# Gated group norms ahead of a column scan: the group statistics about the last mean, a shorter reciprocal root, copies in pieces, more filler matmuls

## The reference

```python
def gated(v, cfc_w, bn_w, bn_b):          # layers 0 to 2: x = x + gated(gn(x), ...)
    mean, mx, std = mean(v), max(v), std(v, ddof=1)      # over the 1024 pixels of a channel
    u = stack([mean, mx, std], -1)                       # 4 x 1024 x 3
    med = median(u.reshape(4, -1), axis=-1)              # of 3072 values per image
    z = einsum('bck,ck->bc', (u - med) ** 3, cfc_w)
    g = sigmoid(z / sqrt(1 + 1e-5) * bn_w + bn_b)
    return v * g

def scan(v, conv_w, conv_b, a):           # layer 3: x = x + scan(gn(x), ...)
    # forward, then backward over the 32 columns:
    # cur = prelu(Wc @ prev + conv_b) + column, Wc 1024 x 1024
```

## Time and profile before

| | us |
|---|---|
| median of 3 runs | 903.53 |
| lowest and highest | 901.96, 905.42 |
| profiled execution | 902.32 |
| its span in the profile | 900.6 |
| loading and first statistics | up to 57.9 |
| gated layers with the last group norm | 57.9 to 144.2 |
| column scan | from 144.2 |

### The profile page before, as it was taken

The page is one execution under the profiler, slowest core; times in us unless marked ns, Lnnn a source line. Parts: engine busy times, 40 slices in busy tenths (PEclk is TensorE's granted clock), DMA queues, the critical chain, the costliest instruction groups (busy, mean ns, idle before and its releaser), DMA issues.

```text
span 900.6 us, 13037 instructions
## 1 busy us (share of the span) xinstructions
PE 807.3 (90%) x3699; PEld 632.0 (70%) x3699; DVE 688.5 (76%) x1410; ACT 433.8 (48%) x1380; POOL 36.3 (4%) x68
## 2 busy tenths in 40 slices
PE   0055569999999999999999999999999999999996
PEld 0022226888888888888888888888888888888885
DVE  7987777677666766776667678877887887788887
ACT  6974441444444444444444444444444444444444
POOL 2002430000000000000000000000000000000002
PEclk9996667999999999999999999999999999999998
DMA  8940020000000000000000013333222333332223
GB/s 349 421 166 1 0 94 24 1 0 0 0 0 0 0 0 0 0 0 0 0 0 0 0 47 93 93 93 93 87 72 74 93 93 93 93 93 80 72 80 116
DMA packets 71513, 56.79 MB, mean 63 GB/s; under 512 B 1872, under 2 KB 67408, under 8 KB 69456
## 3 DMA queue, kind: packets, MB, share of 16 engines
q1 hardware_dynamic: 71072, 56.63, 18.9%
q10 hardware_dynamic: 432, 0.07, 0.0%
HBM read 39.91 MB, written 16.78 MB: 63 GB/s over the span
## 4 chain that ended last, share of the span: by engine, by line
PE 85%; DVE 12%; issue 1%; ACT 1%; DMA 1%; ACTq 0%; DVEq 0%
PE ps_prods L544 26%; PE ps_prods L547 25%; PE ps_prods L548 25%; PE ps_turns L556 6%; DVE half_max L624 4%; DVE below_flags L676 3%; DVE bn_parts L619 2%; PE ps_values L511 1%; DMA x_sb<-x_cols 1%; DVE under L682 0%; DVE x_sb L774 0%; PE ps_second L492 0%; DVE t L606 0%; DVE rstd L608 0%; DVE t L607 0%
## 5 line engine op out<-in xcount | busy, mean ns | idle before, releaser
L544 PE MATMUL ps_prods<-w_hi,s_hi 128*128 128x512 f32 x992 | 402.3, 406 | 0.5 <-DVE s_lo L764 0.5
L547 PE MATMUL ps_prods<-w_lo,s_hi 128*128 128x512 f32 x992 | 401.4, 405 | 0.0
L548 PE MATMUL ps_prods<-w_hi,s_lo 128*128 128x512 f32 x992 | 391.1, 394 | 0.0
L456 ACT ACTIVATE act_buf<-ps_prods 128x256 f32<-128x256 f32 x248 | 81.9, 382 | 358.7 <-PE ps_prods L548 355.7
L774 DVE SCALAR_TENSOR_TENSOR x_sb<-act_buf,x_sb 128x256 f32 (+1 forms) x248 | 107.2, 432 | 156.4 <-ACT act_buf L462 145.8
L544 PEld LDWEIGHTS ps_prods<-w_hi,s_hi 128*128 128x128 f32 x992 | 186.9, 188 | 39.3 <-DVE s_lo L764 1.3
L548 PEld LDWEIGHTS ps_prods<-w_hi,s_lo 128*128 128x128 f32 x992 | 187.2, 189 | 38.4
L547 PEld LDWEIGHTS ps_prods<-w_lo,s_hi 128*128 128x128 f32 x992 | 187.6, 189 | 32.8
L462 ACT ACTIVATE act_buf<-ps_turns,bias 128x128 f32<-128x128 f32 x496 | 157.6, 377 | 50.8 <-PE ps_turns L556 50.8
L468 ACT ACTIVATE ps_below<-ps_turns,neg_bias 128x128 f32<-128x128 f32 x496 | 153.0, 362 | 0.0
L781 DVE SCALAR_TENSOR_TENSOR x_sb<-ps_below,neg_slope,x_sb 128x256 f32 (+1 forms) x248 | 119.3, 481 | 4.9
(11 more groups left out here) (120 smaller groups left out, 320.9 us busy)
## 6 DMA issues: line engine op xcount, KB each, us to landing
x_sb<-x_cols SPq DMA_DIRECT2D x16, 1024.0 KB, 21.3
stage<-x_cols SPq DMA_DIRECT2D x31, 512.0 KB, 4.0
out_cols<-x_sb SPq DMA_DIRECT2D x31, 512.0 KB, 4.8
w_raw<-w_t SPq DMA_DIRECT2D x8, 512.0 KB, 21.3
x_sb<-x_cols SPq DMA_DIRECT2D x1, 2048.0 KB, 8.0
x_sb<-x_cols SPq DMA_DIRECT2D x1, 512.0 KB, 3.8
out_cols<-x_sb SPq DMA_DIRECT2D x2, 256.0 KB, 2.3
params<-gates ACTq DMA_DIRECT2D x1, 60.0 KB, 5.5
```

Source lines behind the costliest of these rows:

```text
L456: act.activation(act_buf[:, half], ps_prod[c][:, half], ACT.Copy).then_inc(raw_copied, 1)
L544: pe.matmul(ps_prod[c], s_hi[:, k, :], w_hi[:, k, w_cols], start=(k == 0), stop=False)
L547: pe.matmul(ps_prod[c], s_hi[:, k, :], w_lo[:, k, w_cols], start=False, stop=False)
L548: return pe.matmul(ps_prod[c], s_lo[:, k, :], w_hi[:, k, w_cols], start=False, stop=(k == CT - 1))
```

## The change

- **Group norm.** The second moment is no longer taken about the new group mean but about the last one, so that mean and second moment come out of one product (64 columns instead of 32), and the variance follows by subtracting the square of the mean's shift. Layer 0 keeps its two products (`first_norm`). The later ones (`next_norm`) scale the centred arrays `cent` by 1 + gate x rstd.
- **Second moment.** Its two squares and their sum, `cent[:, 0]`, are formed in the rounds 0 to 2 of the median search, behind the comparison (L682).
- **rsqrt** has eight dependent operations instead of ten, with other constants.
- **Copies.** ACT and DVE copy the means and maxima in pieces of 2, 2 and 4 channel tiles, and PE transposes means and maxima of a piece in turn; the deviations come last.
- **Small steps.** `under_steps` is one instruction, and `halves` is gone: `fold` is scaled once at the start and `middle` itself is the stationary operand of the last product.
- **POOL.** In every layer one `split_low` now stands between POOL's copy and its wait for the transposes, and one behind that wait.
- **Fillers.** 4 also in round 3, 4 ahead of the tops' product (L529), 1 ahead of the median's (L532), 8 instead of 4 behind it, 2 instead of 1 in layer 0's group norm.

The diff, cut to its core (declarations of tiles are left out):

```diff
...
-        def copies(k, c0):
+        def copies(k, c0, c1):
...
+        SPLITS = [(0, 2), (2, 4), (4, CT)]
...
                 pool.wait_ge(unit_ready, 2 * layer + 2)
-                pool.tensor_copy(*copies(2, 4)).then_inc(pool_copied, 1)
+                pool.tensor_copy(*copies(2, 4, CT)).then_inc(pool_copied, 1)
+                split_low()
                 pool.wait_ge(spread_high, layer + 1)
-                if layer > 0:
-                    split_low()
                 split_low()
...
-                for c0 in (0, 4):
-                    act.activation(*copies(0, c0), ACT.Copy).then_inc(act_copied, 1)
+                for c0, c1 in SPLITS:
+                    act.activation(*copies(0, c0, c1), ACT.Copy).then_inc(act_copied, 1)
...
+                if layer == 0:
+                    pe.matmul(ps_means, group_ones[:, :], cent[:, 1, :, :].rearrange(flat), start=True, stop=True)\
+                        .then_inc(means_given, 1)
+                    keep_warm(2, ps_warm)
...
+                else:
+                    pe.matmul(ps_pair, group_ones[:, :], grown[:, :, :, :].rearrange("p a n c -> p (a n c)"),
+                              start=True, stop=True).then_inc(means_given, 1)
                 if layer == LAYERS:
                     break
                 keep_warm(8, ps_warm)
...
+                for k, (c0, c1) in [(k, piece) for piece in SPLITS for k in range(2)] + [(2, (0, 4)), (2, (4, CT))]:
...
                     pe.matmul(ps_cell, blocks_bf[:, :], under[:, :], start=True, stop=True).then_inc(cells_counted, 1)
-                    if k < ROUNDS - 2:
-                        keep_warm(4, ps_second)
+                    keep_warm(4, ps_second)
...
                           start=False, stop=True).then_inc(floors_ready, 1)
+                keep_warm(4, ps_warm)
                 pe.wait_ge(tops_ready, layer + 1)
...
+                keep_warm(1, ps_warm)
                 pe.wait_ge(median_ready, layer + 1)
-                pe.matmul(ps_med, ones[0:2 * N, :], halves[:, :], start=True, stop=True)\
+                pe.matmul(ps_med, middle[:, 0:1].broadcast_to([2 * N, P]), fold[:, :], start=True, stop=True)\
                     .then_inc(median_spread, 1)
-                keep_warm(4, ps_warm)
+                keep_warm(8, ps_warm)
...
-                link(dve.tensor_scalar(out.bitcast(i32), a.bitcast(i32), -0.5, float(0x5F3759DF), ALU.mult, ALU.add))
-                for _ in range(3):
-                    link(dve.tensor_tensor(u, out, out, ALU.mult))
-                    link(dve.scalar_tensor_tensor(v, u, -0.5, a, ALU.mult, ALU.mult))
-                    link(dve.scalar_tensor_tensor(out, v, 1.5, out, ALU.add, ALU.mult))
+                link(dve.tensor_scalar(out.bitcast(i32), a.bitcast(i32), -0.5, float(0x5F1FFFF9), ALU.mult, ALU.add))
+                link(dve.tensor_tensor(u, out, out, ALU.mult))
+                link(dve.scalar_tensor_tensor(v, u, -THIRD * FIRST_PULL, a, ALU.mult, ALU.mult))
+                link(dve.scalar_tensor_tensor(out, v, THIRD * FIRST_PULL * FIRST_SPAN, out, ALU.add, ALU.mult))
+                link(dve.tensor_tensor(u, out, out, ALU.mult))
+                link(dve.scalar_tensor_tensor(v, u, -1.0 / THIRD ** 2, a, ALU.mult, ALU.mult))
+                link(dve.scalar_tensor_tensor(u, v, 10.0 / 3.0, v, ALU.add, ALU.mult))
+                link(dve.scalar_tensor_tensor(out, u, 5.0, out, ALU.add, ALU.mult))
...
-            dve.tensor_tensor(fold[:, :], ident[0:2 * N, 0:N], ident[0:2 * N, N:2 * N], ALU.add)
...
+            link(dve.tensor_tensor(fold[:, :], ident[0:2 * N, 0:N], ident[0:2 * N, N:2 * N], ALU.add))
+            dve.tensor_scalar(fold[:, :], fold[:, :], -0.5, None, ALU.mult)
...
+            def next_norm(layer):
+
+                by_two = grow[:, :, :].unsqueeze(1).broadcast_to([P, 2, N, CT])
+                link(dve.tensor_tensor(grow[:, :, :], gate[:, :, :], group_rstd, ALU.mult))
+                link(dve.scalar_tensor_tensor(grown[:, :, :, :], by_two, 1.0, cent[:, 0:2, :, :], ALU.add, ALU.mult))
+                dve.scalar_tensor_tensor(grown[:, 0, :, :], grow[:, :, :], 1.0, grown[:, 0, :, :], ALU.add, ALU.mult)\
+                    .then_inc(means_asked, 1)
+                dve.tensor_tensor(pulled[:, :, :], pull[:, :, :], grow[:, :, :], ALU.mult)
+                link(dve.tensor_tensor(scaled[:, :, :], a_scale[:, :, :], grow[:, :, :], ALU.mult))
+                dve.tensor_tensor(pull[:, :, :], pull[:, :, :], pulled[:, :, :], ALU.add)
+                dve.scalar_tensor_tensor(cent[:, 2:4, :, :], by_two, 1.0, cent[:, 2:4, :, :], ALU.add, ALU.mult)
                 dve.wait_ge(means_given, layer + 1)
...
+                link(dve.tensor_scalar(t2[:, 0, :, :], means, 1.0, None, ALU.mult))
+                link(dve.scalar_tensor_tensor(t1[:, 0, :, :], t2[:, 0, :, :], -1.0, t2[:, 0, :, :], ALU.mult, ALU.mult))
+                link(dve.scalar_tensor_tensor(group_var, t1[:, 0, :, :], GN_EPS, squares, ALU.add, ALU.add))
+                dve.tensor_tensor(a_scale[:, :, :], a_scale[:, :, :], scaled[:, :, :], ALU.add)
+                dve.tensor_tensor(a_shift[:, :, :], a_shift[:, :, :], pulled[:, :, :], ALU.add)
+                dve.tensor_tensor(pull[:, :, :], pull[:, :, :], means, ALU.subtract)
+                if layer < LAYERS:
+                    dve.tensor_tensor(cent[:, 1, :, :], grown[:, 1, :, :], means, ALU.subtract)
+                    dve.tensor_tensor(cent[:, 2, :, :], cent[:, 2, :, :], means, ALU.subtract)
+                rsqrt(group_rstd, group_var, t1[:, 0, :, :], t2[:, 0, :, :])
...
+                        if layer > 0 and k == 0:
+                            dve.tensor_tensor(t1[:, 0, :, :], cent[:, 1, :, :], cent[:, 1, :, :], ALU.mult)
...
-                for upper in range(2):
-                    ins = dve.scalar_tensor_tensor(under_steps[:, upper, :], excess[:, :].broadcast_to([P, N]),
-                                                   float(upper), last_step[:, :], ALU.is_le, ALU.mult)
-                ins.then_inc(below_ready, 1)
+                dve.scalar_tensor_tensor(under_steps[:, :, :], ranks[:, :, :], excess[:, 0:1], last_step[:, :, :],
+                                         ALU.is_ge, ALU.mult).then_inc(below_ready, 1)
...
-                for c0 in (0, 4):
-                    dve.tensor_copy(*copies(1, c0)).then_inc(dve_copied, 1)
+                for c0, c1 in SPLITS:
+                    dve.tensor_copy(*copies(1, c0, c1)).then_inc(dve_copied, 1)
```

More of the change, by code:

```diff
@@ L95, in gated_norm_and_column_scan_kernel @@
         mean_var = tmp("mean_var", [P, N, CT, 2])
-        stat = tmp("stat", [P, N, NSTAT, CT])
+        cent = tmp("cent", [P, 1 + NSTAT, N, CT])
+        grown = tmp("grown", [P, 2, N, CT])
         unit = tmp("unit", [P, N, NSTAT, CT])
@@ L130, in gated_norm_and_column_scan_kernel @@
         scaled = tmp("scaled", [P, N, CT])
+        pulled = tmp("pulled", [P, N, CT])
         scratch.close()
@@ L431, in _ @@
                 act.wait_ge(unit_ready, 2 * layer + 1)
-                for c0 in (0, 4):
-                    act.activation(*copies(0, c0), ACT.Copy).then_inc(act_copied, 1)
+                for c0, c1 in SPLITS:
+                    act.activation(*copies(0, c0, c1), ACT.Copy).then_inc(act_copied, 1)
                 act.wait_ge(unit_ready, 2 * layer + 2)
-                act.activation(*copies(2, 0), ACT.Copy).then_inc(act_copied, 1)
+                act.activation(*copies(2, 0, 4), ACT.Copy).then_inc(act_copied, 1)
                 act.wait_ge(spread_low, layer + 1)
@@ new lines, in _, with first_norm @@
+            link(dve.tensor_tensor(fold[:, :], ident[0:2 * N, 0:N], ident[0:2 * N, N:2 * N], ALU.add))
+            dve.tensor_scalar(fold[:, :], fold[:, :], -0.5, None, ALU.mult)
+            def first_norm():
+                dve.wait_ge(means_given, 1)
+                means = ps_means.rearrange("p (n c) -> p n c", n=N)
+                link(dve.tensor_tensor(cent[:, 1:3, :, :], cent[:, 1:3, :, :],
+                                       means.unsqueeze(1).broadcast_to([P, 2, N, CT]), ALU.subtract))
+                link(dve.tensor_tensor(t2[:, 0, :, :], cent[:, 1, :, :], cent[:, 1, :, :], ALU.mult))
+                dve.scalar_tensor_tensor(cent[:, 0, :, :], plane_var, (PIX - 1.0) / PIX, t2[:, 0, :, :],
+                                         ALU.mult, ALU.add).then_inc(vars_asked, 1)
+                dve.tensor_scalar(pull[:, :, :], means, -1.0, None, ALU.mult)
+                dve.wait_ge(vars_given, 1)
+                link(dve.tensor_scalar(group_var.rearrange("p n c -> p (n c)"), ps_var, GN_EPS, None, ALU.add))
+                both = "p a n c -> p (a n c)"
+                rsqrt(*(t[:, :, :, :].rearrange(both) for t in (rstd, var, t1, t2)))
+                link(dve.tensor_tensor(cent[:, 3, :, :], plane_var, plane_rstd, ALU.mult))
@@ L683, in median @@
                                                  ALU.mult, ALU.is_ge).then_inc(under_ready, 1)
```

(19 more changed lines are left out.)

102 lines of the change are left out of this document (42 added, 60 removed).

## The result

| | before | after |
|---|---|---|
| median, first comparison, 9 runs each | 904.23 us | 901.56 us |
| ratio to before, 95% interval | | 0.9981 (0.9972 to 0.9990) |
| ratio in a second comparison (12 and 23 runs) | | 0.9970 (0.9960 to 0.9981) |
| profiled execution, its span | 902.32, 900.6 | 903.03, 901.3 |
| first product of the scan | 145.90 | 143.57 |

The change makes the kernel 0.2 to 0.3% faster: by the ratios 1.7 to 2.7 us, where 4.1 were forecast. The ratio is the comparison's own estimate and not the quotient of the medians, which lie 2.67 and 3.05 us apart (0.9970 and 0.9966). With 901.56 us the result lies under the forecast's upper bound of 902, and between its 899.0 for faster and its 908.0 for slower, to which it had given 0.41. The profiled execution is the slowest of its nine (900.78 to 903.03) and shows two of the losses in full.

A forecast was written before the change was run, and what follows sets the result against it. Outside PE's untouched column scan, it took the gated layers' string of short steps, half at 1.2 GHz, as the bound. From 902.32 us: -2.4 - 0.5 - 1.05 - 1.05 + 1.0 - 0.1 = -4.1, so 898.2, range 894.5 to 902.

The forecast's parts named there:

- part 6, the fillers and the clock: PE's fillers: shorter products against delayed ones and a possible slow scan start, -0.1 us, bounds -1.5 and +4.5.
- Norms of layers 1 and 2, and the last: Gate to `unit`: one 64-column product and fewer steps, -0.72 at each of two boundaries, -0.94 at the last, -2.4 us together.
- Layer 0's norm: Layer 0's group norm: two linked root steps of 64 elements go, -0.5 us, bounds -0.5 and -0.3.
- Median tail: End of the median, three times: one `under_steps` saves 0.08 and dropping `halves` 0.27, -1.05 us in all.
- I expect the rise somewhere in the tail: Clock rises between the tops' product and the fourth of the last eight fillers; group products -0.7 us, half of six products -0.7.
- POOL behind the transposes: Layers 1 and 2: one split behind the transposes ends the first comparison's stall, twice -0.52, -1.05 us.
- The copies: Copies before the transposes: POOL's split holds up DVE's third copy, PE waits, +0.34 a layer, +1.0 us.
- The fall before the scan: Clock falls in PE's gap after the warm-ups, eight scan products run at 1.2 GHz: +1.6 us, given one half, +0.8.
- the slower rival: Clock falls after the group product, layers transposed at 1.2 GHz: +2.9 a layer, two 904.0, three 907.0 us; chance 0.08.
- the fillers run cold: Clock does not rise until most of the eight fillers are through: in full 902.2 us, half 900.5; chance 0.20.
- All three signs that the prediction named as wrong: Granted 0.50 during transposes, or in the scan's first step, or over 0.1 us between a ready semaphore and L529's successor.
- The argument on the median's distance from the profiled run: Nothing added: layers transposed before the clock's rise would explain runs up to 905.42 us, and the new order makes that rarer.

The follow-up runs named there:

- e1: Changed kernel with the filler counts of the kernel before, everything else as changed: 899.27 us, ratio 0.9941.
- e5: Kernel before with the changed kernel's filler counts and nothing else: 907.63 us, ratio 1.0037.
- e7: Changed kernel with 8 fillers per round, 15 behind layers 1 and 2's group products, 20 scan warm-ups, POOL's early split only in layer 0: 895.73 us, ratio 0.9907.
- e10: Kernel before with all the fillers of e7 and nothing else: 900.71 us, ratio 0.9976.
- e6: Kernel before with only the changed order of POOL's splits, in every layer: 902.33 us, ratio 0.9989.
- e9: e7 with POOL's early split back in every layer: 895.69 us, ratio 0.9924.
- e2: Changed kernel with POOL's early split only in layer 0, one split behind the transposes in layers 1 and 2: 900.36 us, ratio 0.9954.
- e3: Changed kernel with 20 instead of 11 warm-up matmuls ahead of the scan: 900.80 us, ratio 0.9958.
- e4: Changed kernel without the four fillers ahead of the tops' product: 900.95 us, ratio 0.9965.
- e8: e7 with 6 instead of 8 fillers in each round: 895.15 us, ratio 0.9914.

## Why the prediction was wrong

The direction, the interval (894.5 to 902, its upper end just) and the mechanisms of parts 1 to 5 were right, but the size was not: -4.1 against -1.7 to -2.7. The step that failed is part 6, the fillers and the clock. The forecast put it at -0.1; taken out of the changed kernel (e1) and put into the kernel before (e5) the extra fillers cost 2.6 and 3.3 us. Parts 1 to 5, forecast at -4.0, are what e1 has, and it gained 5.3 by ratio and 4.5 by the start of its scan. Step by step, in the first profile:

1. **Norms of layers 1 and 2, and the last.** Right. From the sigmoid's start to `unit` 4.52 (83.62 to 88.14) against 5.49, -0.97 twice, and -1.24 at the last: -3.2. Forecast -2.4 and the products' 0.7, -3.1. The added `cube` copy ahead of `grow` costs 0.10, which was overlooked; the 64-column product is as cheap as taken.
2. **Layer 0's norm.** -0.4 against -0.5: here the first product took 0.63 and not 0.41, the length that such a product has elsewhere at a granted 0.50, though the windows from 57 to 60 read 1.00.
3. **Median tail, with L529's share of part 6. Here most of the miss lies.** Forecast: -1.05 for the instructions, -0.7 for shorter products, +0.5 for fillers in the way, -1.2 together. Measured: the tail is 0.21, 0.27 and 0.27 longer, +0.75. "I expect the rise somewhere in the tail" was too early. The clock rose at about 81.9, 109.2 and 136.5, when L541 was through and L545 as well but for its second half in layer 0, so all three L541 were late by 0.45 (forecast: half of three by 0.35), of the six products one gained 0.06, and the filler ahead of L545 cost another 0.1. Nor did the single `under_steps` save its 0.08: L730 takes 0.225 where the two had 0.24. With the old filler counts (e1) and with the clock held (e7 against e10) the instructions alone gain 0.26 a layer, -0.8 and not -1.05. The miss is 1.95 us; with it the forecast would have been -2.15, between the two comparisons.
4. **POOL behind the transposes.** Right: -1.05, shown by e6 (-1.0).
5. **The copies.** Right for the layers 1 and 2: from the copies' start to the first count 3.95 us against 3.64, +0.31 (forecast +0.34); the hold-up itself is shown by e9. The third copy took the 1.50 us that the prediction asked for, and the gap was 0.38 and not 0.5. Wrong for layer 0, where POOL's split waited its turn (1.45 us) and the transposes ended 0.29 earlier.
6. **The clock.** The rise in time for the group product came three times. The fall before the scan cost 1.6 in the first profile and nothing in the second, as the half given to it says. The fall before the transposes, priced as the slower rival, came in one layer of the first profile (4.62 us instead of 3.44 with the gap), and in both later layers of e2 and e3: +1.1 to 1.7 a layer, and not 2.9, since the clock rose again before they ended or just then.

Sum of the first profile: -0.4 - 3.2 + 0.75 - 1.05 + 0.0 (copies of layers 0 and 1) + 1.5 (layer 2's transposes, their gap included) = -2.4, and the scan starts 2.33 earlier. With 1.6 in the scan -0.7 remain; the other 1.4 between the spans is the scan's longer length. By ratio it is -1.7 to -2.7.

Of the rivals, "the fillers run cold" (0.20) is the nearest to what came in the tail, and "slower" to what came in layer 2; neither came whole. The terms given for the first, 1.4, 0.5 and 2.7, add up to 902.8 and not to its 902.2. All three signs that the prediction named as wrong are in the first profile: a granted 0.50 during transposes, one in the scan's first step, and 0.49 us between the ready tops and L541.

The argument on the median's distance from the profiled run went wrong too: the new order makes a fall at the transposes of the layers 1 and 2 more frequent and not rarer. In the profiles with the new counts (the changed kernel twice, e2, e3, e5) it came in 6 of 10 such layers, in those with the old counts (the kernel before twice, e6, e1) in none of 8. The same eight fillers last 1.89 us at 2.4 GHz (84.98 and 111.22 in the changed kernel) and leave PE idle for 2.00 and 2.01 before the transposes, where at 1.2 GHz they took 3.40 and 3.47 and left 0.32 and 0.24 (the kernel before). That the extra fillers as such turned a 5 us gain into 2 to 3 is shown by e1 and e5 together. What is not separated is how the five places share that cost, beyond e4.

## What to carry to other kernels

A filler delays what stands behind it in PE's order (L541 here by 0.49 us). Price fillers at the lower clock and place them by the higher: count what they delay at the 0.43 us each that they took at 0.50, and what gap they leave at the 0.21 each that they took at 1.00. Either hold the clock through the whole stretch, in every gap (e7, e8), or keep the fillers few and out of the way of the chain (e1); the measure between them cost more than it gave here. A kernel without any filler was not run. Where two engines hold each other up, as DVE's copies and POOL's subtraction did here, an operation split in more pieces offers more places to be passed (of two copies the longest took 0.83, of three the last 1.50), so put the other engine's long work where nobody asks.

## What the runs showed of the hardware

- PE's granted clock stayed at 1.00 through the rounds of e7 and e9 (eight fillers in each) and of e8 (six). It fell once during those of e10 (eight; 0.50 from 98 to 101), and during the rounds in the profile of every kernel with four (in the changed kernel at 75, 99 and 126). What it goes by, the runs don't show.
- 24 float32 transposes took 2.84 to 2.93 us at 2.4 GHz without a wait for a copy (e9's layer 0, layer 2 before), and up to 4.63 with most of them at 1.2 GHz (e3).
- DVE's copy of 512 elements took 0.41 in the layers 1 and 2 of e7, where no subtraction of POOL's ran beside it, and 1.50 behind POOL's 1.3 us subtraction in layer 1 of the changed kernel, which had started 0.10 ahead of it (89.13 and 89.23); in layer 0 of the changed kernel the copy was 0.51 ahead of the subtraction (63.19 and 63.70), took 0.83 behind POOL's copy, and the subtraction took 1.45 and not 1.26. Each time it was the instruction that started behind one of the other engine that took longer; what the two engines share, no run shows.
- The same scan took 754.7 us in some executions and 756.0 in others, 0.17%, nearly as much as the change was worth in the first comparison. All four profiles on one chip had the short length, and those on two other chips the long one but for e5; the cause is open.
